# The numbers 0 to 127 are read from PSUM instead of SBUF in the two sum passes of a four-layer graph network, and the edge attributes use one PSUM bank per step instead of two

## The reference, cut to what matters

```
h = relu(layernorm(x))                                   # layer 3
agg[src] += h[dst] + edge_attr_16 @ W_edge + b_edge      # plus a self loop per node
x = x + (relu(batchnorm(agg @ W1 + b1)) @ W2 + b2)
h = relu(layernorm(x))                                   # layer 4
agg[dst] += (h @ W + b)[src] + edge_attr_6 @ We + be
x = x + relu(agg)
```

## Time and profile before

| | |
|---|---|
| time, median of three runs | 21892.74 us (21871.51 to 21898.50) |
| span of the profiled execution | 15054.0 us |
| instructions | 271220 |
| PE, DVE, ACT, POOL busy | 58%, 65%, 19%, 74% of the span |
| src sum pass, first to last gather | 10721.8 to 12786.9 us |
| dst sum pass, first to last gather | 12952.0 to 15005.4 us |

### The profile page before, as it was taken

How to read it: one execution, slowest core, us unless ns; L and a number is a source line. 1 busy time by engine, 2 the same in 40 slices (tenths; PEclk the granted TensorE clock), 3 DMA queues, 4 the chain that set the end, 5 groups by cost and what they waited for, 6 DMA issues and landing times. The chain is left out here.

```text
span 15054.0 us, 271220 instructions
## 1 busy us (share of the span) xinstructions
PE 8740.4 (58%) x56159; PEld 6734.5 (45%) x56575; DVE 9778.7 (65%) x34050; ACT 2787.6 (19%) x7303; POOL 11087.4 (74%) x11347
## 2 busy tenths in 40 slices
PE   6766667777777777555555555555444444544444
PEld 2212226666666666244444444444333333433334
DVE  8877777777878778866666677777533333433334
ACT  0011114444444444421111111111100000200000
POOL 4777767777777777777777777777677777477776
PEclk8866668999999999865555555555555555655555
DMA  2011122222222222422222222222222222422222
GB/s 85 7 42 50 53 59 74 69 69 69 69 69 69 69 69 67 152 83 59 59 58 59 58 63 63 62 63 63 69 63 63 63 62 60 121 59 59 58 59 68
DMA packets 734382, 992.39 MB, mean 66 GB/s; under 512 B 271737, under 2 KB 534898, under 8 KB 732626
## 3 DMA queue, kind: packets, MB, share of 16 engines
q0 software_dynamic: 387968, 670.55, 17.1%
q1 hardware_dynamic: 324786, 301.13, 6.5%
q10 hardware_dynamic: 20000, 3.33, 0.1%
HBM read 795.25 MB, written 178.86 MB: 65 GB/s over the span
## 5 line engine op out<-in xcount | busy, mean ns | idle before, releaser
L1834 DVE TENSOR_TENSOR acc<-banks,acc 128x128 f32 x3328 | 969.8, 291 | 2616.2 <-PE banks L1792 2247.3
L668 POOL DMA_INDIRECT rec_dst<-stage_dst_sort,row_dst_sort x1563 | 1575.4, 1008 | 641.1 <-issue 474.3
L800 POOL DMA_INDIRECT far_att<-table_qv,recs_att x1664 | 1636.5, 983 | 523.9 <-issue 506.8
L800 POOL DMA_INDIRECT far_sum_dst<-table_h,recs_dst x1613 | 1561.2, 968 | 584.1 <-issue 491.7
L800 POOL DMA_INDIRECT far_sum_src<-table_h,recs_src x1613 | 1572.9, 975 | 558.8 <-issue 491.6
L800 POOL DMA_INDIRECT far_rel_src<-table_xw,recs_rel_src x1638 | 1574.7, 961 | 508.7 <-issue 494.2
L800 POOL DMA_INDIRECT far_rel_dst<-table_xw,recs_rel_dst x1638 | 1561.1, 953 | 510.4 <-issue 494.5
L1622 DVE TENSOR_TENSOR acc<-banks,acc 128x128 f32 x3328 | 969.7, 291 | 1119.2 <-PE banks L1548 1002.5
L936 POOL DMA_INDIRECT rec_src<-moved_att,row_src x1248 | 1245.0, 998 | 397.3 <-issue 379.9
L1792 PE MATMUL banks<-far_sum_src,hot_sum_src 128*128 128x128 f32 x3226 | 825.1, 436 | 1214.9 <-DVE hot_sum_src L1825 831.3
L1792 PE MATMUL banks<-far_sum_dst,hot_sum_dst 128*128 128x128 f32 x3226 | 825.9, 436 | 1147.5 <-DVE hot_sum_dst L1825 899.8
(11 more groups left out here) (343 smaller groups left out, 21302.0 us busy)
## 6 DMA issues: line engine op xcount, KB each, us to landing
lone_sync_rel_dst<-table_xw SPq DMA_DIRECT2D x3328, 0.5 KB
lone_sync_rel_src<-table_xw SPq DMA_DIRECT2D x3328, 0.5 KB
lone_sync_sum_src<-table_h SPq DMA_DIRECT2D x3328, 0.5 KB
lone_sync_sum_dst<-table_h SPq DMA_DIRECT2D x3328, 0.5 KB
lone_scalar_sum_src<-table_h ACTq DMA_DIRECT2D x3200, 0.5 KB
lone_scalar_sum_dst<-table_h ACTq DMA_DIRECT2D x3200, 0.5 KB
table_xw<-xw_rel_tables SPq DMA_DIRECT2D x98, 512.0 KB
far_att<-table_qv,recs_att POOLq DMA_INDIRECT x1664
```

The source lines that it names most:

```text
L668: e.indirect_dma_start(out=flat_dst, out_offset=bass.IndirectOffsetOnAxis(ap=row["dst"][:, c + i:c + i + 1], axis=0), in_=stage["dst"][:, ...
L800: e.indirect_dma_start(out=self.far[:, g % RING, t, :], out_offset=None, in_=table, in_offset=bass.IndirectOffsetOnAxis(ap=index, axis=0)) ...
L1834: e.tensor_tensor(acc[:, bass.ds(at[t], 1), :], sums[g0 % 4][:, t:t + 1, :], acc[:, bass.ds(at[t], 1), :], ALU.add).then_inc(k.s_sum, 1)
```

## The change

Three things change in `sum_pass`, for both sides.

1. At the start of each pass DVE copies `k.col` to the first 128 columns of PSUM's bank 5 (`numbers`) and signals the new semaphore `s_iota`. The first DVE instruction behind it waits for that.
2. The one-hot instruction reads `numbers` in place of `k.col`. Its second operand and its output stay in SBUF.
3. So that bank 5 is free, the attribute step uses bank 4 alone for the transposes and bank 6 alone for the products. PE waits for the copy or the sum of the attribute step before this one, where it waited for the one before that. Bank 7 is unused.

```diff
+        k.s_iota = k.sem("s_iota")
...
         def scalar(e):
-                e.copy(et[:, b, 0:m], k.psum[4 + b][0:n_more, 0:m]).then_inc(k.s_et, 1)
+                e.copy(et[:, b, 0:m], k.psum[4][0:n_more, 0:m]).then_inc(k.s_et, 1)
                 if not gine:
                     e.wait_ge(k.s_ec, f0 + j + 1)
-                    e.copy(k.conv[j], k.psum[6 + b][:, 0:m].rearrange("p (n f) -> p n f", f=F)).then_inc(k.s_spent, 1)
+                    e.copy(k.conv[j], k.psum[6][:, 0:m].rearrange("p (n f) -> p n f", f=F)).then_inc(k.s_spent, 1)
...
         def tensor(e):
                 if j is not None:
                     w0, n = WIN4[j]
-                    if j >= 2:
-                        e.wait_ge(k.s_et, f0 + j - 1)
+                    if j >= 1:
+                        e.wait_ge(k.s_et, f0 + j)
                     for i in range(n):
-                        t = e.transpose(k.psum[4 + j % 2][0:n_more, i * P:(i + 1) * P], more[:, w0 + i, :], k.ident[:, :])
+                        t = e.transpose(k.psum[4][0:n_more, i * P:(i + 1) * P], more[:, w0 + i, :], k.ident[:, :])
...
                     e.wait_ge(k.s_et, f0 + j + 1)
-                    if j >= 2:
-                        e.wait_ge(k.s_spent, f0 + j - 1)
+                    if j >= 1:
+                        e.wait_ge(k.s_spent, f0 + j)
                     for i in range(WIN4[j][1]):
-                        t = e.matmul(k.psum[6 + j % 2][:, i * P:(i + 1) * P], et[:, j % 2, i * P:(i + 1) * P], wc[:, :], start=True, stop=True)
+                        t = e.matmul(k.psum[6][:, i * P:(i + 1) * P], et[:, j % 2, i * P:(i + 1) * P], wc[:, :], start=True, stop=True)
...
+        numbers = k.psum[5][:, 0:P]
 
         def vector(e):
             spent = 0
+            e.tensor_copy(numbers, k.col[:, :]).then_inc(k.s_iota, 1)
+            e.wait_ge(k.s_iota, 1 if gine else 2)
             if not gine:
                 e.wait_ge(k.s_par, pars)
...
-                    e.tensor_tensor(hot[:, g3 % HOT, :, :], over(k.col[:, :], GT), st.rows(g3, LOC, LOC + 1).to_broadcast([P, GT, P]),
+                    e.tensor_tensor(hot[:, g3 % HOT, :, :], over(numbers, GT), st.rows(g3, LOC, LOC + 1).to_broadcast([P, GT, P]),
                                     ALU.is_equal).then_inc(k.s_mark, 1)
...
-                        e.tensor_tensor(acc[:, w0:w0 + n, :], acc[:, w0:w0 + n, :], k.psum[6 + j % 2][:, 0:n * P].rearrange("p (n f) -> p n f", f=F),
+                        e.tensor_tensor(acc[:, w0:w0 + n, :], acc[:, w0:w0 + n, :], k.psum[6][:, 0:n * P].rearrange("p (n f) -> p n f", f=F),
                                         ALU.add).then_inc(k.s_spent, 1)
```

## The result

The changed kernel takes 22412.19 us (median of four runs, 22396.12 to 22441.16) against 21895.62 us before (21871.51 to 21903.32). The ratio is 1.0245, 95% interval 1.0232 to 1.0257: 517 us slower, where 76 us faster was forecast.

A forecast was written before the change was run, and what follows sets the result against it. The prediction took POOL's gathers to bound both sum passes. Shorter gathers gave -33.7 us in dst and -42.3 us in src, other terms 0, so 21892.7 - 76.0 = 21816.7 us, range 21780 to 21862.

The forecast's parts named there:

- one unbroken chain of POOL's gathers: Both sum passes: POOL's gathers plus issue time fill the stretch, 1572.9 + 491.6 + 0.6 = 2065.1 us in src.
- A sum pass gets shorter only if POOL's gathers do, and then by the full amount: Both sum passes: time removed from POOL's gathers shortens the span equally, together -76.0 us.
- The 6838.7 us outside the span: Time outside the profiled span of 15054.0 us, with no row; taken as unchanged by the edit.
- a rival with a chance of 0.11: Whole kernel: timed executions do not follow the trace, so the time stays 21893 us; chance 0.11.
- What is late next: Sum passes: single rows from SP and ACT take 65 us for 128, against 77.7 a step; POOL stays the floor.
- The mechanism of the collisions: Sum passes: DVE instructions with two SBUF operands stretch POOL's gathers; removing 832 of them gives -33.7 dst, -42.3 us src.
- the third rival: Sum passes: more lost to collisions in timed executions; at twice the excess -152 us, 21741 us; chance 0.04.
- The counter-rule: POOL's gathers: two-input `tensor_tensor` does not stall descriptor making, so the change would give 0 us.
- The operand's own cost: One-hot instruction on DVE: its length with the PSUM operand stays 0.68 to 0.69 us, no change.
- the single bank: Attribute steps of the sum passes: new waits on one bank are already met or covered; cost 0.
- The copy: Start of each sum pass, DVE's copy to PSUM: 0.3 us, covered by other waits, cost 0.
- The slower rival: Gathers under line 1830: PSUM operand still holds POOL, and longer; +117 us, 22010 us; chance 0.03.

The follow-up runs named there:

- the second one of before: The kernel before, run again with no edit for a second profile: 21883.25 us, ratio 0.9992, span 21902.1 us.

## Why the prediction was wrong, by its own steps

- "... both passes are one unbroken chain of POOL's gathers", and "A sum pass gets shorter only if POOL's gathers do, and then by the full amount": this is the step that failed. It was true in the execution of the earlier trace rows and false in all thirteen later profiles, each as long as its timed runs. In the second one of before POOL waited 1046 and 1007 us for records whose load stands behind 32 single rows in SyncE's queue.
- "The 6838.7 us outside the span have no row. I take them as unchanged": the warning was seen and not followed. A gap of 31% meant that the profile was of another kind of execution, and a rival with a chance of 0.11 was too little. What was no part of any rival is the sign: that for 149 us less of gathers 675 us of waits would come.
- "What is late next": SyncE and ScalarE "at about 0.51 us each" came from the earlier trace rows. In the timed runs a row takes on average 1.15 us of SyncE's queue while POOL gathers (0.87 per us), and 1.6 us after the change (0.62 per us). Three instructions make a row, and every one may take 0.7 us there instead of 0.03 to 0.2. So POOL was not the floor; that queue was.
- The mechanism of the collisions was right. The dst gathers' mean went to 943 ns with a maximum of 961 (forecast 947 or 948, under 1000), the src gathers' to 945 with a maximum of 1236, and long ones are left under the bias sum, as the timeline after has it:

```profile
17016.27 0.69 DVE L1852 TENSOR_TENSOR x<-x,bias_sum_src 128x512 f32<-128x512 f32 x1
17016.58 1.20 POOL L801 DMA_INDIRECT far_sum_src<-table_h,recs_src  x1 [0.30 <-issue]
```

  In the runs the excess was almost twice that of the earlier trace rows: busy time fell by 74 and 75 us, 149 together, where 76 was forecast; 152 was the third rival's figure. It was worth nothing.
- The rule of the Trainium skill on two SBUF inputs, in "SBUF — State Buffer", section "Who interferes with whom", held for the gathers, by those numbers. The counter-rule weighed beside it, that a two-input `tensor_tensor` leaves descriptor making alone, would leave 945 and 991 ns equal; the runs contradict it.
- The operand's own cost was right: the one-hot instruction has a mean of 682 ns after, had 690 and 693. So was the single bank: 21891 against 21892 us with the bank alone. The copy takes 0.29 us, forecast 0.3, and ends ahead of the first gather at 15466.82 us; no run has it alone.

```profile
15466.20 0.29 DVE L1820 COPY banks<-col 128x128 f32<-128x128 f32 x1 [8.59 <-PEq L1688]
...
L1830 DVE TENSOR_TENSOR hot_sum_src<-banks,recs_src 128x512 f32<-128x512 f32 x416 | 283.6, 682 | 1163.9 <-DMA recs_src<-rec_src 1163.1 <-issue 0.8
```

- The slower rival named a longer hold of POOL. The loss came from its opposite, the absence of a hold: SyncE's rate beside the gathers fell from 0.87 to 0.62 rows per us.

The sum with the right terms, from the groups of POOL: gathers -74 - 75 us, waits for records +342 + 333 us, together +526 us, against 527 us by the stretches and 517 by the medians.

## What to carry to other kernels

Compare a profile's span with the timed runs before anything else. Thirteen profiles here agree with their time to 2 us; the one that did not was of an execution unlike the timed ones, and its bound was not the kernel's. Where small DMAs issued by SyncE or ScalarE stand in a queue ahead of loads that others wait for, GpSimd's gathers can slow them, and freeing GpSimd can make this worse: look at the rate of the issues while it gathers and while it waits. Work given to a second queue to spare the first should be timed without it now and then; here the relief for POOL, in the relation and the sum passes together, cost 11% of the kernel.

## What the runs showed of the hardware

- While POOL makes gathers, the single rows of SyncE and ScalarE are slowed, and ScalarE's rows slow SyncE's further. SyncE: 1.59 rows per us with POOL waiting, 0.87 with gathers and pauses by DVE, 0.62 with gathers and none, 1.02 with the pauses by DVE when ScalarE has no rows. The slowing grows over some 16 us of gathers and outlasts them by about 2 us. The Trainium skill says in "DMA: Bandwidth & Descriptors", section "SWDGE vs HWDGE vs iDMA", that DMAs issued by these engines never touch the path of GpSimd's descriptors and are immune to VectorE's hold on it. Nothing here speaks against the immunity from VectorE; that they keep their rate beside GpSimd itself does not follow, and the rows above show that they don't.
- It is not only the issue of a DMA that is held: register instructions on the same sequencer, mostly under 0.04 us, take about 0.7 us there too. In the middle of the src pass that befell 832 of 6318 of them on SyncE after the change, 737 of 6327 before, and none in the execution with a span of 15054 us, where the longest took 0.04 us. What they wait for stays open. No run here tells whether it comes with the recording of the executions or with the chip's own work, and why that one execution had none of it. The page "NOTIFIC — the notification-queue block" of the Trainium skill, section 7.1, has a mechanism by which records that pile up stall an engine; no run here shows it.
- A gather that DVE doesn't touch takes 938 to 961 ns in the dst pass, 1613 times.
- The pace of gathers that keep the ring full was 1.42 us in a pass without single rows, where its instruction and issue take 1.25 to 1.28: a further limit behind POOL's instruction, of which the traces show only late landings or products.
